# A gated linear attention block on one core: VectorE's order of weighing and gating keys, the bank of the turned decay rows, and ScalarE's place for the decay

## The chip, the cores and the metric

One core of one Trainium2 chip runs the whole program in one launch. The metric is device time in microseconds (us), the median of several executions. TensorE is called PE in the profile, with its weight loads as PEld; VectorE is DVE, ScalarE is ACT, GpSimd is POOL and SyncE, which issues most transfers, is SP.

## The reference

The block takes x of 8192 tokens by 512. The first half is normalised, modulated and sent through gated linear attention with 16 heads of 64; the second half is a gated feed-forward layer that mixes each token with the one before it. Only the first half is touched by the change.

```python
h = layernorm(x) * (1 + ca) + sa
q, k, v = h @ Wq.T, h @ Wk.T, h @ Wv.T
log_decay = -softplus(h @ Wd.T + bd)              # one number per token and head
k = k * sigmoid(h @ Wg.T)
s_t = exp(g_t) * s_{t-1} + k_t^T v_t ; o_t = q_t s_t   # per head, a 64 x 64 state
out = rmsnorm(o) * norm_w * sigmoid(h @ Wog.T) @ Wo.T
x = x + ga * out ; then x = x + gb * ffn(layernorm(x) * (1 + cb) + sb)
```

## The kernel before

The program has three parts that follow each other: `prepare` turns and splits the weights, `attention_pass` does everything up to `o`, and `output_pass` does the rest. Products of the projections are made in three passes, since each factor is split into a high and a low part (lines 55, 56 and 57 of the profile).

`attention_pass` works in 32 tiles of 256 tokens (two chunks of 128). Its turn i does two things side by side: the projections of tile i (`proj`), and the recurrence of tile j = i - 1 (`gla`). A turn has eight steps p = 0 to 7, one per pair of heads. Turn 0 has no recurrence (it also makes four modulation vectors), turns 1, 30 and 31 are written out, turns 2 to 29 are one hardware loop, and turn 32 has only the recurrence. So 31 turns have both.

In step p (1 to 7) PE turns the gated keys `kg` of pair p into `psX` (line 606), projects the gate `g` of pair p - 1 of the next tile, and ahead of the last quarter of that projection it waits in `ready()` for what the small products of the recurrence need, `kw` of pair p among it (`kv_ready`). Then come the small 64 x 64 products `weigh_v`, the state's increments, the scores and `add_held` (lines 570, 639, 648, 581), and then the projections of `q` and `k` of pair p - 1. The projections use the two banks `psJ` in turn, so each waits until the one two before it was read: `q` waits for DVE's reading of the `k` before it (`gate_k`, line 843), and `k` waits for ACT's reading of `g` (`copy_g`, line 720).

Each engine runs its own instructions in the order in which they are written; semaphores join them. DVE's step is `dve_tile`: `kw` (line 914, the turned keys weighed by a decay), `grow_q` (line 852), three `mid` and one `state` (line 929), `prob` (line 934), `sum_o` (line 889), and at the end `gate_k` of pair p - 1. ACT's step is `act_tile`: four exponentials (line 764), a copy of the state (`keep_state`, line 746), `copy_g`, `copy_o`, `copy_q`.

The decay of the next tile is made late in the turn. In step 6 PE sums the log decays into `psC` (lines 612 and 614), ACT makes `w_new` of it in `turn_decay` (lines 738 and 739), and PE turns two parts of `w_new` into rows, `psN`, inside the projection of `k` (line 538). DVE copies these rows out (line 954), SP stores them, and in step 7 reads them back, spread over the partitions, for the next turn (`spread_rows`, `grow_rows`). `psN` lies in `psP`, the banks from which DVE also reads `psO`; hence this wait of PE ahead of the projection of `k` in step 6:

```python
if p == 6:
    pe.wait_ge(s["w_new"], i + 1)
    if gla:
        hold(pe, s["o"], n)
project(i, "k", p - 1, pe, p == 6)
```

Of the kernel before, what the change touches and what calls it, by code (L numbers as in the profile page):

```python
# [26 lines left out]
H = 16  # L27
DH = HID // H
TOK = 8192
CH = 128  # L30
NC = 2
# [3 lines left out]
NP = HID // P  # L35
# [310 lines left out]
def attention_pass(nc, t, W, norm, h_parts, next_jobs, stage, h_next, h_loaded, wmod_v, x_v, o_v, h_v, cum_v, cum_b):  # L346
    with ExitStack() as ctx:  # L347
# [11 lines left out]
        o = sb("o", [P, 2, NC, CH])  # L359
# [28 lines left out]
        psP = ps("psP", [P, 2, 4, CH])  # L388
        psO, psN = psP[:, :, 0, :], psP[0:2 * NC * H, 0, 1, :]
        psJ = [ps(f"psJ{n}", [P, 512]) for n in range(2)]  # L390
        psT = ps("psT", [P, KD, T])
        psH = psP[:, :, 3, :]
        psC = psT[:, 1, NC * H:5 * NC * H]
        psM = psP[:, 1, 2, 0:KD]
# [45 lines left out]
        def grow_rows(sp, i, p):  # L440

            hold(sp, s["qg"], NP * i + p - 1)
            sp.dma_start(grown[:, p % 2, :],
                         cum_b[i, 1, 2 * p:2 * p + 2, :].unsqueeze(1).to_broadcast([2, DH, T])
                         ).then_inc(grow[p % 2], 16)
# [12 lines left out]
        def sp_tile(sp, i, gla, proj, prep, opens=False):  # L458
            j = i - 1
            for p in range(NP):  # L460
# [12 lines left out]
                if p == 7 and proj:  # L473
                    sp.wait_ge(s["n_rows"], 32 * (i + 1))
                    for pair in range(4):
                        spread_rows(sp, i, pair)
                    for pair in range(2):
                        grow_rows(sp, i, pair)
                if gla and (p > 0 or not opens):
                    store_o(sp, j if p else j - 1, (p - 1) % NP)  # L480
# [61 lines left out]
        def turn_x(pe, n):  # L542
            pe.wait_ge(s["xn"], NC * (n + 1))
            hold(pe, s["hT"], KD * n)
            hold(pe, s["w_new"], n - 1)
            for k in range(KD):
                for c in range(NC):
                    last = nc.tensor.transpose(psT[:, k, c * CH:(c + 1) * CH], x[:, c, k * P:(k + 1) * P],
                                               t["ident"][:, :])
                last.then_inc(s["xT"], 1)  # L550
# [43 lines left out]
        def pe_tile(pe, i, gla, proj, prep, opens=False):  # L594
            j = i - 1
            for p in range(NP):
# [22 lines left out]
                def ready():  # L619
                    if follows:  # L620
                        if p == 7 and proj:
                            pe.wait_ge(s["n_out"], i + 1)
                        o_ready(pe, n - 1)
                    kv_ready(pe, j, p)
# [34 lines left out]
                if p > 0 and proj:  # L659
                    project(i, "q", p - 1, pe)  # L660
                    if p == 6:
                        pe.wait_ge(s["w_new"], i + 1)
                        if gla:
                            hold(pe, s["o"], n)
                    project(i, "k", p - 1, pe, p == 6)
# [87 lines left out]
        def act_tile(act, i, gla, proj, prep, opens=False):  # L753
            j = i - 1
            for p in range(NP):
                n = NP * j + p
                if gla:
                    act.wait_ge(s["mask"], n + 1)
# [8 lines left out]
                    keep_state(act, j, p)  # L767
                    if p == 6 and proj:
                        turn_decay(act, i)
                    if p == 1:  # L770
# [122 lines left out]
        def dve_tile(dve, i, gla, proj, prep, opens=False):  # L893
            j = i - 1
            for p in range(NP):
# [13 lines left out]
                if gla:  # L909
                    if p == 0:  # L910
# [6 lines left out]
                        w_cur[:, 2, :, 2 * p:2 * p + 2].unsqueeze(3).to_broadcast([P, NC, 2, DH]),  # L917
                        ALU.mult).then_inc(s["kw"], 1)
                    grow_q(dve, j, p)
                    if not proj and p >= 3:  # L920
# [39 lines left out]
                if p == 5 and prep > 1:  # L960
                    norm_x(dve, i + 2)
                if p > 0 and proj:
                    gate_k(dve, i, p - 1)
            if proj:
                dve.wait_ge(s["w_new"], i + 1)
                hold(dve, s["state"], NP * i)
# [520 lines left out]
```

## Time and profile before

| what | value |
|---|---|
| time, median of 3 runs | 3450.75 us (3449.19 to 3459.34) |
| profiled execution, its own time | 3447.54 us |
| span of its trace | 3445.8 us |
| granted TensorE clock, mean over the span | 0.987 of full speed |
| busy: PE, DVE, ACT, POOL | 3288.3, 1888.0, 1308.6, 463.8 us |

The span is the time from the first to the last record of the trace, and 1.7 us of the profiled execution's own time lie outside it. Times in the rows below are counted from the start of the span. The attention part runs from about 46 us to about 2138 us; its turns 2 to 29 are about 64 us long each. Turn 4, from which most rows are taken, begins at 287.4 us and ends at 351.6 us.

### The profile page before, as it was taken

To read this page: it belongs to the slowest core of one execution; us is meant where nothing else is said; L and a number is where in the kernel's file an instruction comes from. 1 tells how busy PE (TensorE), PEld (TensorE's weight loads), DVE (VectorE), ACT (ScalarE), POOL (GpSimd) and SP (SyncE) were. 2 spreads that over 40 slices of the span, in tenths; PEclk is the share of its full clock that TensorE was granted. 3 is DMA by queue.
4 is the path that set the end of the run, shared out by engine and by line. 5 is a ranking of instruction groups with operands and counts; after the bars stand their busy time and mean duration, and the time that the engine had idled before them with its cause. 6 is when DMAs were issued, how large, how long until landed. Compare 5 with 4: busy or idle time off the path is not lost. (4 is left out here: it accounts for less than half of the span.)

```text
span 3445.8 us, 99642 instructions
## 1 busy us (share of the span) xinstructions
PE 3288.3 (95%) x37253; PEld 3015.9 (88%) x37253; DVE 1888.0 (55%) x4825; ACT 1308.6 (38%) x3584; POOL 463.8 (13%) x723
## 2 busy tenths in 40 slices
PE   7999999999999999999999997999999999999998
PEld 6888888898898888888888896888999988999887
DVE  6444444444444444444444445577676677676676
ACT  4344344344344344344344344323333323333322
POOL 0111101101111111101101111211121111121110
PEclk9999999999999999999999998999999999999999
DMA  5221221221221221221221224332222332222330
GB/s 202 80 83 64 84 80 62 76 89 63 84 81 63 81 83 64 84 80 62 77 88 62 83 70 144 98 85 73 73 77 81 87 84 73 73 78 80 87 83 25
DMA packets 273382, 279.77 MB, mean 81 GB/s; under 512 B 24720, under 2 KB 221344, under 8 KB 273072
## 3 DMA queue, kind: packets, MB, share of 16 engines
q1 hardware_dynamic: 270960, 270.67, 26.0%
q8 instruction: 290, 4.75, 0.6%
q10 hardware_dynamic: 2112, 4.19, 0.4%
q14 instruction: 20, 0.16, 0.0%
HBM read 189.84 MB, written 84.93 MB: 80 GB/s over the span
## 5 line engine op out<-in xcount | busy, mean ns | idle before, releaser
L55 PE MATMUL psJ<-h_hi,w_g_hi 128*128 128x256 f32 x1024 | 320.9, 313 | 36.5 <-DVE qg L852 30.5
L55 PE MATMUL psJ<-h_hi,w_q_hi 128*128 128x256 f32 x1024 | 309.1, 302 | 0.0
L55 PE MATMUL psJ<-h_hi,w_k_hi 128*128 128x256 f32 x1024 | 292.0, 285 | 12.4 <-DVE o L889 10.9
L929 DVE SCALAR_TENSOR_TENSOR mid<-state,w_all,psB 128x64 f32<-128x64 f32 x256 | 71.8, 280 | 414.5 <-PE psB L648 414.4
L55 PE MATMUL psG<-h_hi,w_og_hi 128*128 128x256 f32 x1024 | 287.6, 281 | 8.2 <-PEq L347 4.7
L57 PE MATMUL psJ<-h_hi,w_k_lo 128*128 128x256 f32 x1024 | 286.7, 280 | 0.0
L56 PE MATMUL psJ<-h_lo,w_g_hi 128*128 128x256 f32 x1024 | 286.7, 280 | 0.0
L56 PE MATMUL psJ<-h_lo,w_q_hi 128*128 128x256 f32 x1024 | 286.6, 280 | 0.0
L57 PE MATMUL psJ<-h_hi,w_q_lo 128*128 128x256 f32 x1024 | 286.4, 280 | 0.0
L56 PE MATMUL psJ<-h_lo,w_k_hi 128*128 128x256 f32 x1024 | 286.1, 279 | 0.0
L57 PE MATMUL psJ<-h_hi,w_g_lo 128*128 128x256 f32 x1024 | 285.8, 279 | 0.0
L56 PE MATMUL psG<-h_lo,w_og_hi 128*128 128x256 f32 x1024 | 284.6, 278 | 0.0
L57 PE MATMUL psG<-h_hi,w_og_lo 128*128 128x256 f32 x1024 | 284.5, 278 | 0.0
L764 ACT ACTIVATE prob<-cum_rows,w_cur 128x64 f32<-128x64 f32 x1024 | 273.6, 344 | 8.7 <-issue 4.9
L843 DVE SCALAR_TENSOR_TENSOR kg<-gate,psJ 128x256 f32<-128x256 f32 x256 | 107.8, 421 | 292.2 <-PE psJ L57 260.6
L55 PE MATMUL psJ<-w_v_hi,h_hi 128*128 128x264 f32 (+1 forms) x768 | 257.2, 335 | 0.4 <-DVE kg L843 0.4
L55 PEld LDWEIGHTS psJ<-h_hi,w_g_hi 128*128 128x128 f32 x1024 | 193.2, 189 | 72.8 <-issue 56.6
L57 PE MATMUL psJ<-w_v_hi,h_lo 128*128 128x264 f32 (+1 forms) x768 | 250.9, 327 | 0.0
L56 PE MATMUL psJ<-w_v_lo,h_hi 128*128 128x264 f32 (+1 forms) x768 | 250.0, 326 | 0.0
L720 ACT ACTIVATE gate<-psJ 128x256 f32<-128x256 f32 x256 | 98.5, 385 | 359.3 <-PE psJ L57 357.9
L751 ACT COPY o<-psP 128x256 f32<-128x256 f32 x256 | 95.1, 372 | 337.1 <-PE psP L581 333.8
L1223 ACT ACTIVATE og<-psG 128x512 f32<-128x512 f32 x128 | 76.7, 600 | 355.4 <-PE psG L57 355.3
(238 smaller groups left out, 9626.7 us busy)
## 6 DMA issues: line engine op xcount, KB each, us to landing
cum_rows<-cum_dram SPq DMA_DIRECT2D x512, 64.0 KB, 2.8
grown<-cum_dram SPq DMA_DIRECT2D x256, 128.0 KB
o_dram<-o SPq DMA_DIRECT2D x256, 128.0 KB, 1.9
o_cols<-o_dram SPq DMA_DIRECT2D x128, 256.0 KB, 5.0
an_norm_x<-in_L_attn_x_dram SPq DMA_DIRECT2D x32, 512.0 KB, 6.4
h_dram<-h_hi SPq DMA_DIRECT2D x32, 512.0 KB, 2.8
h_dram<-h_lo SPq DMA_DIRECT2D x32, 512.0 KB, 4.1
h_hi<-h_dram SPq DMA_DIRECT2D x32, 512.0 KB, 3.9
```

The costliest lines, as they stand in the source:

```text
L55: nc.tensor.matmul(out, w_hi, x_hi, start=first, stop=False)
L56: nc.tensor.matmul(out, w_hi, x_lo, start=False, stop=False)
L57: return nc.tensor.matmul(out, w_lo, x_hi, start=False, stop=last)
L720: nc.scalar.activation(gate[:, b % 2, :], psJ[USES.index(("g", b)) % 2][:, 0:T], ACT.Tanh, scale=0.5).then_inc(s["by_act"], 1)
L751: nc.scalar.copy(o[:, p % 2, :, :], psH).then_inc(s["o_part"], 1)
L764: last = nc.scalar.activation(prob[:, p % 2, 2 * h + c, :], rows_of(p)[:, h, c * DH:(c + 1) * DH], ACT.Exp, bias=w_cur[:, 0, c, 2 * p + h: ...
L843: nc.vector.scalar_tensor_tensor(out=kg[:, b, :], in0=gate[:, b % 2, :], scalar=1.0, in1=psJ[USES.index(("k", b)) % 2][:, 0:T], op0=ALU.ad ...
L929: nc.vector.scalar_tensor_tensor(out=into, in0=mid[:, p % 2, m - 1, :] if m else state[:, p, :], scalar=w_all[:, c, b, p:p + 1], in1=psK[: ...
L1223: nc.scalar.activation(og[:, n % 2, :, :], psG[n % 2][:, :].rearrange("p (b t) -> p b t", b=2), ACT.Sigmoid).then_inc(s["sg"], 1)
```

## The change

Four things change. DVE makes `kw` of pair p first and then gates the keys that PE projected in the step before, in steps 2, 3, 4, 6 and 7; the gating of pair 3 stays at the end of step 4, and those of pairs 6 and 7 at the end of the turn. `psN` moves from `psP` into `psT`, the banks in which x is turned; with it PE's wait for `o` in step 6 and its wait for `n_out` in step 7 go, and `turn_x` gets a wait for `n_out` of the turn before. ACT makes `w_new` ahead of step 6's exponentials in place of behind them and the state's copy. SP issues the reads of `grown` for pairs 0 and 1 between those of `cum_rows`.

```diff
@@ -386,10 +386,11 @@
         psS, psX = psB[:, :, 0, :], psB[:, 0, 2:4, :]
         psK = psB[:, :, 1, :].rearrange("p b (c d) -> p b c d", c=NC)
         psP = ps("psP", [P, 2, 4, CH])
-        psO, psN = psP[:, :, 0, :], psP[0:2 * NC * H, 0, 1, :]
+        psO = psP[:, :, 0, :]
         psJ = [ps(f"psJ{n}", [P, 512]) for n in range(2)]
         psT = ps("psT", [P, KD, T])
         psH = psP[:, :, 3, :]
+        psN = psT[0:2 * NC * H, 2, 0:CH]
         psC = psT[:, 1, NC * H:5 * NC * H]
         psM = psP[:, 1, 2, 0:KD]
 
@@ -472,10 +473,11 @@
                     sp.wait_ge(s["m_sum"], KD * len(MODS))
                 if p == 7 and proj:
                     sp.wait_ge(s["n_rows"], 32 * (i + 1))
-                    for pair in range(4):
+                    for pair in range(2):
                         spread_rows(sp, i, pair)
-                    for pair in range(2):
                         grow_rows(sp, i, pair)
+                    for pair in range(2, 4):
+                        spread_rows(sp, i, pair)
                 if gla and (p > 0 or not opens):
                     store_o(sp, j if p else j - 1, (p - 1) % NP)
                 if not proj and p == 0:
@@ -543,6 +545,7 @@
             pe.wait_ge(s["xn"], NC * (n + 1))
             hold(pe, s["hT"], KD * n)
             hold(pe, s["w_new"], n - 1)
+            hold(pe, s["n_out"], n - 1)
             for k in range(KD):
                 for c in range(NC):
                     last = nc.tensor.transpose(psT[:, k, c * CH:(c + 1) * CH], x[:, c, k * P:(k + 1) * P],
@@ -618,8 +621,6 @@
 
                 def ready():
                     if follows:
-                        if p == 7 and proj:
-                            pe.wait_ge(s["n_out"], i + 1)
                         o_ready(pe, n - 1)
                     kv_ready(pe, j, p)
 
@@ -660,8 +661,6 @@
                     project(i, "q", p - 1, pe)
                     if p == 6:
                         pe.wait_ge(s["w_new"], i + 1)
-                        if gla:
-                            hold(pe, s["o"], n)
                     project(i, "k", p - 1, pe, p == 6)
                 if p == 4 and proj:
                     for b in range(4):
@@ -754,6 +753,8 @@
             j = i - 1
             for p in range(NP):
                 n = NP * j + p
+                if p == 6 and proj and gla:
+                    turn_decay(act, i)
                 if gla:
                     act.wait_ge(s["mask"], n + 1)
                     hold(act, s["gla"], n - 1)
@@ -765,8 +766,6 @@
                                                         bias=w_cur[:, 0, c, 2 * p + h:2 * p + h + 1], scale=-1.0)
                     last.then_inc(s["e"], 1)
                     keep_state(act, j, p)
-                    if p == 6 and proj:
-                        turn_decay(act, i)
                     if p == 1:
                         copy_v(act, j, 5)
                 if p > 0 and proj:
@@ -916,6 +915,9 @@
                         psX.rearrange("p c (h d) -> p c h d", h=2),
                         w_cur[:, 2, :, 2 * p:2 * p + 2].unsqueeze(3).to_broadcast([P, NC, 2, DH]),
                         ALU.mult).then_inc(s["kw"], 1)
+                if proj and p > 1 and p != 5:
+                    gate_k(dve, i, p - 2)
+                if gla:
                     grow_q(dve, j, p)
                     if not proj and p >= 3:
                         rest_w(dve, p - 3)
@@ -959,9 +961,10 @@
                     norm_stats(dve, i + 2)
                 if p == 5 and prep > 1:
                     norm_x(dve, i + 2)
-                if p > 0 and proj:
+                if p == 4 and proj:
                     gate_k(dve, i, p - 1)
             if proj:
+                gate_k(dve, i, NP - 2)
                 dve.wait_ge(s["w_new"], i + 1)
                 hold(dve, s["state"], NP * i)
                 for h in range(2):
```

On DVE, in step 2 of a turn of the loop, these rows stand before: first the `kg` of the next tile's pair 0 and then the `kw` of pair 2, and `qg`.

```order
L840 ISA
L841 ISA [waits a_by_act]
L843 SCALAR_TENSOR_TENSOR kg<-gate,psJ 128x256 [waits a_score,a_proj]
L912 REGISTER_ALU
L914 TENSOR_TENSOR kw<-psB,w_cur 128x256 [waits a_inc,a_kT]
L849 REGISTER_ALU
L850 ISA [waits a_by_act]
L852 TENSOR_TENSOR qg<-q,grown 128x256 [waits a_gla,a_grow0]
```

After the change the same place reads:

```order
L911 REGISTER_ALU
L913 TENSOR_TENSOR kw<-psB,w_cur 128x256 [waits a_inc,a_kT]
L839 ISA
L840 ISA [waits a_by_act]
L842 SCALAR_TENSOR_TENSOR kg<-gate,psJ 128x256 [waits a_score,a_proj]
L848 REGISTER_ALU
L849 ISA [waits a_by_act]
L851 TENSOR_TENSOR qg<-q,grown 128x256 [waits a_gla,a_grow0]
```

The row of `kw` has moved ahead of that of `kg`; `qg` stays the third.

On ACT, in step 6 of a turn of the loop, these rows stand before. `prob` are the exponentials, `held` is the state's copy, `w_new` the decay, `gate` is what `copy_g` writes.

```order
L733 COPY q<-psJ 128x256 [waits a_qg,a_score,a_proj]
L758 REGISTER_ALU
L764 ACT_TABLE_LOAD [waits a_gla]
L764 ACTIVATE prob<-cum_rows,w_cur 128x64 [waits a_mask]
L764 ACTIVATE prob<-cum_rows,w_cur 128x64 x3
L746 COPY held<-state 128x64 [waits a_gla,a_state]
L738 ACTIVATE w_new<-psT 128x32 [waits a_cur,a_cum]
L739 ACTIVATE w_new<-psT 128x128
L718 REGISTER_ALU
L45 REGISTER_ALU [waits a_proj]
L720 ACTIVATE gate<-psJ 128x256 [waits a_k]
```

After the change, from the same place:

```order
L732 COPY q<-psJ 128x256 [waits a_qg,a_score,a_proj]
L737 ACTIVATE w_new<-psT 128x32 [waits a_cur,a_cum]
L738 ACT_TABLE_LOAD
L738 ACTIVATE w_new<-psT 128x128
L759 REGISTER_ALU
L765 ACTIVATE prob<-cum_rows,w_cur 128x64 [waits a_gla,a_mask]
L765 ACTIVATE prob<-cum_rows,w_cur 128x64 x3
L745 COPY held<-state 128x64 [waits a_gla,a_state]
L717 REGISTER_ALU
L45 REGISTER_ALU [waits a_proj]
L719 ACTIVATE gate<-psJ 128x256 [waits a_k]
```

The two rows of `w_new`, with the wait for PE's sums (`a_cum`), have moved from behind `held` to ahead of the exponentials, and the load of the activation table has moved with them: it stands between the two.

In turn 0, which makes the modulation vectors, DVE's rows of steps 1 and 2 stand like this before. `m_sums` is a sum over weight rows of 128 x 512, and `kg` here is pair 0.

```order
L865 SCALAR_TENSOR_TENSOR m_sums<-m_rows,c_silu_c,m_sums 128x512 [waits a_m_sum] x3
L843 SCALAR_TENSOR_TENSOR kg<-gate,psJ 128x256 [waits a_proj,a_by_act]
L871 COPY c_mod<-psP 128x4 [waits a_m_read]
L876 TENSOR_SCALAR sign<-c_mod 128x4 [waits a_m_out]
L877 SCALAR_TENSOR_TENSOR sign<-c_mod 128x4
L880 TENSOR_SCALAR sign<-sign 128x4 [waits a_gate]
L881 TENSOR_SCALAR sign<-sign 128x4
L883 TENSOR_TENSOR c_ga<-sign 128x4 [waits a_gate]
L862 TENSOR_SCALAR m_sums<-cum_rows,c_silu_c 128x512 [waits a_m_read,m_loaded1,a_gate]
L865 SCALAR_TENSOR_TENSOR m_sums<-cum_rows,c_silu_c,m_sums 128x512 [waits a_m_sum] x3
L843 SCALAR_TENSOR_TENSOR kg<-gate,psJ 128x256 [waits a_proj,a_by_act]
```

After the change:

```order
L864 SCALAR_TENSOR_TENSOR m_sums<-m_rows,c_silu_c,m_sums 128x512 [waits a_m_sum] x3
L870 COPY c_mod<-psP 128x4 [waits a_m_read]
L875 TENSOR_SCALAR sign<-c_mod 128x4 [waits a_m_out]
L876 SCALAR_TENSOR_TENSOR sign<-c_mod 128x4
L879 TENSOR_SCALAR sign<-sign 128x4 [waits a_gate]
L880 TENSOR_SCALAR sign<-sign 128x4
L882 TENSOR_TENSOR c_ga<-sign 128x4 [waits a_gate]
L861 TENSOR_SCALAR m_sums<-cum_rows,c_silu_c 128x512 [waits a_m_read,m_loaded1,a_gate]
L864 SCALAR_TENSOR_TENSOR m_sums<-cum_rows,c_silu_c,m_sums 128x512 [waits a_m_sum] x3
L842 SCALAR_TENSOR_TENSOR kg<-gate,psJ 128x256 [waits a_proj,a_by_act]
```

The `kg` of pair 0 has moved from ahead of the second sum `m_sums` to behind it. The same happens in steps 5 and 6 with the `kg` of pair 4.

## Rows read from the trace of the kernel before

**Rows 1.** The page, its first part: busy time, share of the span, instructions.
```profile
PE 3288.3 (95%) x37253; PEld 3015.9 (88%) x37253; DVE 1888.0 (55%) x4825; ACT 1308.6 (38%) x3584; POOL 463.8 (13%) x723
```

**Rows 2.** PE's waits, 290 to 2055 us: total us, times, longest.
```profile
PE psB L606 <- issue: 52.2, 25, 2.6
PE psJ L55 <- DVE qg L852: 26.8, 55, 0.5
PE psJ L55 <- DVE o L889: 10.1, 26, 0.4
```

**Rows 3.** Timeline, PE's weight loads, step 2: start, us, engine, line, what.
```profile
303.04 0.19 PEld L56 LDWEIGHTS psJ<-h_lo,w_g_hi 128*128 128x128 f32 x1
303.16 0.19 PEld L57 LDWEIGHTS psJ<-h_hi,w_g_lo 128*128 128x128 f32 x1
303.49 0.19 PEld L55 LDWEIGHTS psJ<-h_hi,w_g_hi 128*128 128x128 f32 x1
```

**Rows 4.** Timeline, PE and DVE, step 2 of the same turn.
```profile
302.12 0.38 PE L606 MATMUL psB<-c_ident,kg 128*128 128x128 f32 x2
...
302.31 0.42 DVE L843 SCALAR_TENSOR_TENSOR kg<-gate,psJ 128x256 f32<-128x256 f32 x1 [1.34 <-PE psJ L57]
302.65 0.42 DVE L914 TENSOR_TENSOR kw<-psB,w_cur 128x256 f32<-128x256 f32 x1
```

**Rows 5.** Timeline, PE and DVE, turn 32, where no keys are gated.
```profile
2099.93 0.38 PE L606 MATMUL psB<-c_ident,kg 128*128 128x128 f32 x2
...
2100.35 0.42 DVE L914 TENSOR_TENSOR kw<-psB,w_cur 128x256 f32<-128x256 f32 x1 [0.72 <-PE psB L606]
```

**Rows 6.** Timeline, DVE and PE's weight loads, step 6.
```profile
337.08 0.41 DVE L889 TENSOR_TENSOR o<-o,psP 128x256 f32<-128x256 f32 x1
...
336.96 0.19 PEld L57 LDWEIGHTS psJ<-h_hi,w_q_lo 128*128 128x128 f32 x1
337.73 0.19 PEld L55 LDWEIGHTS psJ<-h_hi,w_k_hi 128*128 128x128 f32 x1 [0.59 <-issue]
```

**Rows 7.** Groups, 290 to 2055 us: busy, mean ns, idle before, releaser.
```profile
L55 PEld LDWEIGHTS psJ<-h_hi,w_k_hi 128*128 128x128 f32 x872 | 165.3, 190 | 15.5 <-issue 15.5
```

**Rows 8.** Timeline, PE and ACT, step 6.
```profile
332.84 0.41 PE L614 MATMUL psT<-g_half,c_ones 128*128 128x64 f32 x2
...
331.04 0.37 ACT L733 COPY q<-psJ 128x256 f32<-128x256 f32 x1 [0.32 <-PE psJ L57]
331.43 1.28 ACT L764 ACT_TABLE_LOAD   x1
332.72 1.07 ACT L764 ACTIVATE prob<-cum_rows,w_cur 128x64 f32<-128x64 f32 x4
333.70 0.23 ACT L746 COPY held<-state 128x64 f32<-128x64 f32 x1
...
333.92 0.26 ACT L739 ACTIVATE w_new<-psT 128x128 f32<-128x128 f32 x1
334.79 0.39 ACT L720 ACTIVATE gate<-psJ 128x256 f32<-128x256 f32 x1 [0.61 <-PE psJ L57]
```

**Rows 9.** Timeline, DVE and PE's weight loads, turn 0.
```profile
56.30 2.33 DVE L865 SCALAR_TENSOR_TENSOR m_sums<-cum_rows,c_silu_c,m_sums 128x512 f32<-128x512 f32 x3
...
56.04 0.19 PEld L55 LDWEIGHTS psJ<-h_hi,w_q_hi 128*128 128x128 f32 x1
...
81.79 0.42 DVE L843 SCALAR_TENSOR_TENSOR kg<-gate,psJ 128x256 f32<-128x256 f32 x1
...
82.64 2.33 DVE L865 SCALAR_TENSOR_TENSOR m_sums<-cum_rows,c_silu_c,m_sums 128x512 f32<-128x512 f32 x3
...
84.43 0.19 PEld L55 LDWEIGHTS psJ<-h_hi,w_q_hi 128*128 128x128 f32 x1
```

**Rows 10.** Windows: stretch, us, busy of five engines, granted clock, DMA share, GB/s.
```profile
416.90:420.30 3.40, 3.40 (x10) 2.55 (x8) 0.43 (x1) 0.00 (x0) 0.00 (x0) 0.52 0.24 74
1840.30:1843.70 3.40, 3.40 (x10) 2.62 (x9) 0.82 (x2) 0.00 (x0) 0.00 (x0) 0.51 0.29 79
```

## The prediction

> **What bounds the kernel now.** I read the page first: PE is busy for 95% of the span and every other engine for 55% or less [rows 1]. So the time is PE's work plus what PE waits for, and a change that leaves its products alone can only win back waits. The view of PE's waits says which they are in the hardware loop [rows 2]: a stop at the loop's restart that nothing in the profile ends (52.2 us), 55 waits named after `qg` (two a turn, in steps 1 and 5, where DVE does other work ahead of `kw`), and 26 of 0.4 us named after DVE's `sum_o`, one a turn. The change touches the last kind. It does not touch the restart, nor steps 1 and 5, whose order on DVE stays.
>
> That view misses short stops, because it takes each product as busy for 0.28 us although the next starts after 0.12. The timeline of the weight loads shows them: they come 0.12 us apart, and in step 2 one comes at 303.49 where 303.28 was due [rows 3], a stop of 0.21 us ahead of the last quarter of the projection of `g`, where PE waits for `kw`. Steps 3, 4 and 7 have the same. In step 6 the first load of the projection of `k` comes at 337.73 where 337.08 was due, 0.65 us late [rows 6].
>
> **The change part by part. PE's wait for `o` in step 6** goes. `sum_o` ends at 337.49 and the load follows at 337.73, so 0.24 us is what a hand-over from DVE to this load takes [rows 6]. With `psN` in another bank, only the decay and ACT's reading of `g` are left to wait for. The decay was ready at 334.18 [rows 8], the rest is below. If neither is late, the whole 0.65 us is won. It is no feature of one turn: the weight loads of `k` stand idle for 15.5 us ahead of their start between 290 and 2055 us, 0.57 us in each of 27 turns [rows 7], and a load's own 0.19 less the spacing of 0.12 makes it 0.64. For 31 turns: 31 x 0.65 = 20.2 us.
>
> **`kw` ahead of `kg` in steps 2, 3, 4 and 7.** In step 2 the two turning products start at 302.12, `kg` occupies DVE from 302.31, and `kw` starts at 302.65, 0.53 us behind the products [rows 4]. Where no keys are gated, `kw` starts 0.42 us behind them [rows 5]. So `kw` is held up for 0.11 us by `kg`, not for its whole 0.42, because the turning itself lasts nearly as long. The stop of 0.21 us shrinks by that and does not vanish; unrounded the two rows differ by slightly more, and I take 0.12. 31 x 4 x 0.12 = 14.9 us. The bounds are 0 (the wait is ended by something other than `kw`, so 0 us) and 0.21 (it ends the stop, 26 us); the hand-over is the nearer evidence. In step 6 the small sums of the decay come between the turning and the projection and cover `kw`, so nothing is won there. `kg` itself comes 0.34 us later and `qg` 0.2 us; `kg` is needed by the projection of `q`, which comes behind the rest of `g`'s and all the small products, and `qg` in the next step, so both cost nothing.
>
> **ACT makes the decay ahead of the exponentials.** This is where something can be lost, since ACT now waits for PE's sums. Before, it loaded the table at 331.43, right behind the copy of `q`, while it had nothing else to do, and the exponentials, the state's copy, the decay and `gate` followed [rows 8]. After, the load stands behind an instruction that waits for the sums. The last of the two L614 products starts about 0.14 us behind the row's 332.84, and with 0.3 us from a product's start to the reader's (as from the second turning product, 0.11 behind 2099.93, to `kw` at 2100.35 [rows 5]) that instruction starts at 333.3. It takes 0.19 us, the load 1.28, so the second starts near 334.8, the exponentials near 334.95, the state's copy near 335.93 and `gate` near 336.06, ending at 336.45, in place of 335.18. PE wants it for the bank of the projection of `k`, due at 337.08; less the hand-over of 0.24 there are 0.39 us to spare. DVE waits for the state's copy ahead of `mid`: it ends at 336.16, which makes `prob` of step 6 about 0.6 us late, near 337.8, and PE asks for it only behind the projection of `k`, after 338.5. So I cost this edit at nothing, and the cover is 0.39 us thin.
>
> The Trainium skill, on its page "ScalarE: Activation LUTs", section "What ACT_TABLE_LOAD costs", puts a switch of tables at 1283 ns plus a drain of about 1380 ns. The load in the trace takes 1.28 us, which agrees, but the exponentials start 0.01 us behind it and it starts 0.02 us behind the copy of `q`, so no drain of that size stands beside it here [rows 8].
>
> **Turn 0 loses.** There DVE gates pair 0 behind a sum over weight rows. That sum ends at 58.63, `kg` would end 0.33 later at 58.96, and with 0.24 for the hand-over PE can load `q` at 59.20; it did at 56.04 [rows 9]. 3.2 us. Pair 4: the sums start at 81.79 in place of `kg`'s, end 0.33 earlier than before at 84.64, `kg` ends at 84.97, PE loads at 85.21 in place of 84.43: 0.8 us. Between them DVE's row of pair 1 may cost some 0.2. Together 4.2 us, once.
>
> **`grown` ahead of `cum_rows` on SP.** Two issues move ahead by some transfers, so `qg` of step 0 is earlier. PE's waits name no such transfer in any turn [rows 2], since step 1 waits for the low part of h, which follows the last projection of `v`. Pair 1's rows are read one issue later and have a step to spare. Nothing. The waits for `n_out`, moved by a turn, were long over: nothing. The transfers that DVE's copy of the decay rows releases start 0.65 us earlier within the turn, ahead of a whole turn's use.
>
> **Sum.** 20.2 + 14.9 - 4.2 = 30.9 us. From the profiled execution's 3447.5 this gives 3416.6. That execution lay 3.2 us under the median, so from the median it is 3419.9. I say 3418, between the two.
>
> **The rivals.** First, **`kw` was not what the short stop waited for**: then it stays, the gain is 20.2 - 4.2 = 16.0, the time 3434. For it: the profile names `qg` in steps 1 and 5, not `kw`. Against: `qg` of that step isn't needed until the next one, and the distances fit `kw`.
>
> Second, the mirror of it: **the stop goes altogether**, 26 in place of 14.9, time 3407. For it: `kw` ends 0.11 us earlier and the restart after a stop may be cheaper. Against: 0.1 us is left by the rows.
>
> Third, **ACT is late in step 6 after all**. Each tenth beyond the 0.39 us costs 3.1 us. If as much as one more load's time, 1.28 us, stood in the chain, PE would stop for 0.89 us: 27.6 us, and the time would be 3446, no change. By the skill's 1.38 us of drain it would be 31 x 0.99 = 30.7, about 3449.
>
> Fourth, **slower**: the same mechanism with the table loaded twice round the moved instructions, 2.56 us more. Then PE stops for 2.17 us a turn, 67 us, and the time is 3485. It decides from a lateness of 0.39 + 1.34 = 1.7 us on. Against it: the built order shows one load a turn in step 6, as before.
>
> Fifth, **the clock**. After some restarts of the loop the granted clock falls to 1.2 GHz, as at 416.9 and 1840.3, the first and last of 8 among 27 [rows 10]. A stretch of 3.4 us at half of 2.4 GHz gives back at most 1.7 us. The stop ahead of it isn't changed, so I expect as many; three more or fewer are 5 us either way, which is in the range. If all 27 restarts fell so, 32 us would be lost and the gain with it.
>
> **How the numbers follow.** The forecast has 0.60. No gain from `kw` 0.12, the whole stop 0.09, ACT late by about a load 0.08, ACT late by more 0.03, the clock 0.03, something else, mostly near no change, 0.05. The range goes from the whole stop (3407, less some noise) to no gain from `kw` with a few us of the clock: 3405 to 3438. A measurement of this kernel tells 0.3%, 10.4 us, from no change, so faster means under 3440. Faster: 0.60 + 0.12 + 0.09 and, of ACT late by a load, the clock and the rest (0.16 together), the 0.07 in which only part of the gain is lost, 0.88; same: the other 0.09; slower: 0.03.
>
> **What would show it.** In the profile after: no wait of PE on `sum_o` ahead of `k`; the weight load of `k` in step 6 0.12 us behind the one before; `kw` 0.42 us behind the first turning product and ahead of `kg`; the short stop in step 2 about 0.1 us; ACT's table load behind the sums and `gate` ending some 0.6 us ahead of that load; `grown` no longer waited for as long by DVE; a stop of about 3 us in turn 0 ahead of `q`. Wrong would be a wait of PE for `gate` in step 6, or a gap in step 2 as long as before.

## The result and the profile after

The changed kernel takes 3459.1 us (median of 20 runs, 3452.9 to 3464.4), the kernel before beside it 3452.9 us (20 runs). The ratio is 1.0018, with a 95% interval of 1.0011 to 1.0025: a loss of 6 us, small but clear of the noise, where a gain of 31 us was forecast.

The page's row of busy times after the change (engine, busy us, share of the span, instructions), to be held against [rows 1]:

```profile
PE 3291.0 (95%) x37253; PEld 3028.0 (88%) x37253; DVE 1873.0 (54%) x4825; ACT 1301.1 (38%) x3584; POOL 464.1 (13%) x723
```

PE's waits of the changed kernel, 290 to 2055 us (total us, times, longest):

```profile
PE psB L609 <- issue: 70.0, 26, 3.2
PE psJ L55 <- DVE qg L851: 25.8, 55, 0.5
```

The wait for `o` is gone, as forecast, and `qg` stands where it stood. The stop at the loop's restart, which the forecast left alone, has grown from 52.2 to 70.0 us [rows 2].

The steps that were priced did happen. Timeline of the changed kernel, step 6 of turn 4, ACT, DVE and PE's weight loads, to be read beside [rows 6, 8]:

```profile
339.44 0.20 ACT L737 ACTIVATE w_new<-psT 128x32 f32<-128x32 f32 x1 [1.83 <-PE psT L617]
339.65 1.28 ACT L738 ACT_TABLE_LOAD   x1
340.94 0.28 ACT L738 ACTIVATE w_new<-psT 128x128 f32<-128x128 f32 x1
341.11 1.05 ACT L765 ACTIVATE prob<-cum_rows,w_cur 128x64 f32<-128x64 f32 x4
342.07 0.23 ACT L745 COPY held<-state 128x64 f32<-128x64 f32 x1
342.20 0.38 ACT L719 ACTIVATE gate<-psJ 128x256 f32<-128x256 f32 x1
...
343.11 0.19 PEld L57 LDWEIGHTS psJ<-h_hi,w_q_lo 128*128 128x128 f32 x1
343.23 0.19 PEld L55 LDWEIGHTS psJ<-h_hi,w_k_hi 128*128 128x128 f32 x1
```

The weight load of `k` follows 0.12 us behind the last of `q`; it was 0.77. ACT's `gate` ends at 342.58, 0.65 us ahead of that load: the chain that the forecast drew for ACT (0.63 expected) holds.

In step 2 (timeline, PE's weight loads and DVE, beside [rows 3, 4]):

```profile
308.68 0.38 PE L609 MATMUL psB<-c_ident,kg 128*128 128x128 f32 x2
...
309.10 0.42 DVE L913 TENSOR_TENSOR kw<-psB,w_cur 128x256 f32<-128x256 f32 x1 [1.56 <-PE psB L609]
...
309.73 0.19 PEld L57 LDWEIGHTS psJ<-h_hi,w_g_lo 128*128 128x128 f32 x1
309.95 0.19 PEld L55 LDWEIGHTS psJ<-h_hi,w_g_hi 128*128 128x128 f32 x1
```

`kw` starts 0.42 us behind the turning products, where it took 0.53, and the last quarter's first load is 0.10 us late in place of 0.21.

**Where the time went.** I split each turn of the hardware loop, in the trace, into the stop at the restart (from the start of the last product of a turn to that of the first of the next), the head (from there to `turn_x`, about 7 us) and the rest, and took means over the 27 restarts (26 turns for the rest):

| us | stop | head | rest | turn | falls of the clock |
|---|---|---|---|---|---|
| before | 2.34 | 7.59 | 54.76 | 64.67 | 8 |
| after | 2.96 | 8.58 | 53.48 | 65.02 | 26 |

A fall is a restart with a stretch at the lower granted clock (1.2 GHz) that begins between 1.2 us ahead of the stop's end and 3 us behind it. The rest is 1.28 us shorter (forecast: 0.65 + 4 x 0.12 = 1.13). The stop gives back 0.62, and the head 0.99: before, a head without a fall takes 7.2 us on average (7.0 to 7.7), and one with a fall takes 8.6 in both kernels. All these figures, here and below, come from one profiled execution of each kernel; that of the kernel before was 5.4 us shorter than the median of its 20 runs. Between the two profiled executions: 28 x 1.28 = 35.8 us won in the loop and 4.8 in turns 1, 30 and 31; lost are 27 x 0.62 = 16.7 at the stops, 27 x 0.99 = 26.7 in the heads, and 7.1 in turn 0. That sums to 9.9 us slower; the spans differ by 9.7.

### The profile page after: what moved, and what is told of

It reads as the page before. It is cut to its first block and busy times, and to the rows that moved or that the text cites. A ratio compares the mean times of both kernels' runs of the same rounds, so it can differ in the third digit from the quotient of the medians.

```text
span 3455.5 us, 99585 instructions
## 1 busy us (share of the span) xinstructions
PE 3291.0 (95%) x37253; PEld 3028.0 (88%) x37253; DVE 1873.0 (54%) x4825; ACT 1301.1 (38%) x3584; POOL 464.1 (13%) x723
## 5 line engine op out<-in xcount | busy, mean ns | idle before, releaser
L55 PE MATMUL psJ<-w_v_hi,h_hi 128*128 128x264 f32 (+1 forms) x768 | 268.9, 350 | 0.4 <-DVE kg L842 0.4
L57 PE MATMUL psJ<-w_v_hi,h_lo 128*128 128x264 f32 (+1 forms) x768 | 260.8, 340 | 0.0
L56 PE MATMUL psJ<-w_v_lo,h_hi 128*128 128x264 f32 (+1 forms) x768 | 260.6, 339 | 0.0
L913 DVE TENSOR_TENSOR kw<-psB,w_cur 128x256 f32<-128x256 f32 x256 | 108.2, 423 | 247.0 <-PE psB L609 247.0
```

Of the source, the lines that this page charges most:

```text
L55: nc.tensor.matmul(out, w_hi, x_hi, start=first, stop=False)
L56: nc.tensor.matmul(out, w_hi, x_lo, start=False, stop=False)
L57: return nc.tensor.matmul(out, w_lo, x_hi, start=False, stop=last)
L913: nc.vector.tensor_tensor(kw[:, :, :].rearrange("p c (h d) -> p c h d", h=2), psX.rearrange("p c (h d) -> p c h d", h=2), w_cur[:, 2, :, 2 ...
```

## The restart of the loop

Timeline of the kernel before at the restart behind turn 4, SP's issues and PE's products:

```profile
341.87 6.25 SPq L436 DMA_DIRECT2D cum_rows<-cum_dram  x8
348.31 1.29 SPq L443 DMA_DIRECT2D grown<-cum_dram  x2
...
349.45 0.28 PE L57 MATMUL psJ<-h_hi,w_k_lo 128*128 128x256 f32 x1
351.56 0.41 PE L606 MATMUL psB<-c_ident,kg 128*128 128x128 f32 x2 [1.83 <-issue]
```

The changed kernel, the restart behind turn 5:

```profile
412.73 1.42 SPq L437 DMA_DIRECT2D cum_rows<-cum_dram  x2
414.40 0.57 SPq L444 DMA_DIRECT2D grown<-cum_dram  x1
415.21 1.43 SPq L437 DMA_DIRECT2D cum_rows<-cum_dram  x2
416.84 0.55 SPq L444 DMA_DIRECT2D grown<-cum_dram  x1
417.57 4.74 SPq L437 DMA_DIRECT2D cum_rows<-cum_dram  x4
...
419.48 0.28 PE L57 MATMUL psJ<-h_hi,w_k_lo 128*128 128x256 f32 x1
422.81 0.41 PE L609 MATMUL psB<-c_ident,kg 128*128 128x128 f32 x2 [3.05 <-issue]
```

"issue" means that no semaphore held PE. What PE waits for shows in the DMA view, as a queue of its own kind. Queues of the kernel before, 348.5 to 351.6 us (packets, MB, share of 16 engines' time):

```profile
q1 hardware_dynamic: 417, 0.29, 30.1%
q8 instruction: 1, 0.02, 2.1%
```

The changed kernel, 418.5 to 421.5 us:

```profile
q1 hardware_dynamic: 401, 0.25, 26.6%
q8 instruction: 1, 0.02, 5.0%
```

At a restart one packet of 16 KB with instructions is fetched. Before it takes 0.021 x 3.1 x 16 = 1.0 us, after 0.050 x 3.0 x 16 = 2.4 us, with no more data moved beside it. Over 27 restarts the first fetch at each takes 0.98 us on average before and 1.58 after, 0.60 more, and the stop is 0.62 longer.

That the stop is this fetch can be read restart by restart. In all 27 restarts of each of the two kernels PE's first product starts 1.63 to 1.80 us behind the end of the fetch (mean 1.70 before, 1.71 after). The fetch begins on average 0.35 us ahead of the turn's last product before and 0.32 after. So only its length differs: 0.88 to 1.30 us before; after the change 2.1 to 2.5 us at 11 restarts, where the stop is 3.1 to 3.5, and 0.9 to 1.6 at the other 16.

What differs is what is in flight: the last read of `grown` is issued 0.4 us ahead of the turn's last product before and 2.6 us ahead of it after (medians of 27). In the 1.5 us ahead of the fetch no packet of 1 KB, the size of `grown`'s, starts at any restart before, and 49 to 72 start at each after. Such a read moves slowly; in the kernel before, 350.0 to 350.9 us, hardly anything else runs (the view's line of the total, then the queue's):

```profile
DMA packets 48, 0.05 MB, mean 50 GB/s; under 512 B 1, under 2 KB 48, under 8 KB 48
...
q1 hardware_dynamic: 48, 0.05, 16.1%
```

48 packets of 1 KB in 0.9 us keep 16.1% of 16 engines, 2.6 of them, busy. `grown` is read with an access pattern whose outermost step counts 2 (two heads, each spread over 64 partitions). The Trainium skill says on its page "DMA: Bandwidth & Descriptors", section "Rules for kernel authors", that the slowest dimension larger than 1 sets how many engines a transfer uses, so that an outermost count of c under 16 keeps it on at most c. The trace agrees in so far as 2.6 of 16 engines are busy with it. That the fetch queues behind such a row of packets on one of these engines is my reading: the trace doesn't name the engine of a packet. The Trainium skill's page "Runtime: NRT & Kernel Launch", section "Instruction fetch mechanics", says that a taken branch to a page that isn't held forces a fetch before execution goes on. The trace agrees: 16 KB are fetched at each restart, and PE stops for 2.34 us on average even in the kernel before.

## The experiments

The expectations name theories by letters: A, that SP's reads start too late and run into the restart; B, that the clock falls by where the restarts lie in time; C, that the order of SP's reads does the harm. Experiments named after_ start from the changed kernel, before_ from the kernel before. The ratio is to the kernel before on the same chip.

**after_sp**: SP's reads in their old order.

```diff
-                    for pair in range(2):
+                    for pair in range(4):
                         spread_rows(sp, i, pair)
+                    for pair in range(2):
                         grow_rows(sp, i, pair)
-                    for pair in range(2, 4):
-                        spread_rows(sp, i, pair)
```

> The changed kernel with SP's order of reads as before (eight of cum_rows, then the two of grown). Theory A (late store): the first read still starts late, so the restart is disturbed as much: 3455 to 3462. Theory C (the order itself: cum_rows as the last reads hurts the instruction fetch, grown does not): the fetch takes 0.9 us again at all restarts and the time falls to about 3430.

Measured 3424.8 us, ratio 0.9912 (0.9892 to 0.9932), 34 us under the changed kernel. PE's waits in it, 290 to 2055 us:

```profile
PE psB L608 <- issue: 53.0, 25, 2.6
```

The stop is 2.38 us, falls 13, the rest 53.55. So the new order on SP, priced at "Nothing", cost all of the expected gain. The expectation had the reason the wrong way round: it blamed the reads of `cum_rows`, and after_split below points at `grown`.

**after_cum**: the store of the decay rows ahead of that of `o`.

```diff
+                if p == 6 and proj:
+                    sp.wait_ge(s["n_out"], i + 1)
+                    for b in range(2):
+                        sp.dma_start(cum_v[i, :, b, :, :], cum_out[:, b * DH:(b + 1) * DH]).then_inc(s["n_rows"], 16)
                 if gla and (p > 0 or not opens):
                     store_o(sp, j if p else j - 1, (p - 1) % NP)
-                if p == 6 and proj:
-                    ...
```

> The changed kernel, but in step 6 SP stores the decay rows ahead of o of the step before, not behind it. Theory A (contention): the stop at the loop's restart grew because SP's reads of cum_rows now run into it; they start late because the store of the decay rows stands directly behind the 128 KB store of o (reads follow 3.4 us behind the store's issue, before 1.4 us). Then the reads start 1 to 2 us earlier, end ahead of the restart as before, the stop falls from 3.0 to 2.3 us a turn and the granted clock falls after fewer restarts: 3459 less 27 x 0.65 = 17 and less up to 1.4 for each fall that stays away: 3415 to 3442. Theory B (phase alone): the clock falls because of where the restarts lie in time, not because of the stop's length: the time stays within 5 us of 3459 unless the turn's length changes.

Measured 3466.4 us, ratio 1.003 (1.0018 to 1.0042); stop 3.12, falls 25. The first read starts 7.4 us ahead of the turn's last product in place of 6.8 (medians of 27), and nothing is won. That is 0.6 us of the 1 to 2 that were expected, so the run speaks against a late store as the cause, but weakly; after_sp and after_split decide.

**after_turn0**: turn 0 gates its keys where it did before.

```diff
-                if proj and p > 1 and p != 5:
+                if proj and gla and p > 1 and p != 5:
                     gate_k(dve, i, p - 2)
 ...
-                if p == 4 and proj:
+                if proj and (p == 4 if gla else p > 0):
                     gate_k(dve, i, p - 1)
             if proj:
-                gate_k(dve, i, NP - 2)
+                if gla:
+                    gate_k(dve, i, NP - 2)
```

> The changed kernel with the gating of keys in turn 0 where it was before. Both theories: turn 0 lasted 66.4 us in place of 59.3; it gets back 7 us, so 3452. Under theory B the later turns may lie otherwise against the clock; a difference beyond 7 us either way speaks for it.

Measured 3452.0 us, ratio 0.999 (0.998 to 1.000): turn 0 is 5.1 us shorter than in the changed kernel (61.3 for 66.4), and a fall follows each of the 27 restarts. Its profiled execution was the slowest of the 12, at 3459.3 us.

**before_psn**: the kernel before with `psN` in `psT` and the waits changed with it, as in the diff of the change; DVE's, ACT's and SP's orders as before.

> The kernel before with only the decay rows moved to the other bank and the waits of PE that go with it. The step 6 stop of 0.65 us a turn goes (20 us), nothing in turn 0, nothing on ACT. If a stop taken from PE is simply won: 3433. Theory A: here sum_o is not late and its store keeps its distance only partly, since the decay rows come 0.6 us earlier and their store moves up to the store of o; so part is lost at the restart: 3430 to 3450. Theory B: depends on the turn's length of about 64.0 less 0.65 us without falls; falls after many restarts and 3440 to 3455.

Measured 3442.4 us, ratio 0.996 (0.9947 to 0.9973). The rest is 53.97, 0.79 us less than before (0.65 forecast); the stop 2.42, falls 17.

**before_sp**: the kernel before with SP's new order alone (the first diff of this section turned round).

> The kernel before with SP's new order of reads alone (grown of pairs 0 and 1 between the reads of cum_rows). Theory C (the order: the second read of grown is now in flight while PE fetches instructions at the loop's restart, a fetch takes 2.2 us in place of 0.9, and the longer stop brings the clock down after nearly every restart): as between after and after_sp, 34 us slower than the kernel before: 3475 to 3495. Rival (the order hurts only together with the decay rows' store, which the bank's move puts right behind the store of o): in the kernel before the reads start 2 us earlier, the reads are over at the restart, and the time stays at 3450 to 3458.

Measured 3456.9 us, ratio 1.001 (1.000 to 1.0019). PE's waits in it, 290 to 2055 us:

```profile
PE psB L607 <- issue: 71.1, 26, 3.2
```

The stop is 3.00 us as in the changed kernel, so the order makes the stop by itself. But only 12 restarts have a fall, and the time rises by 3 us where 27 x 0.66 = 18 would be due and 3475 to 3495 us were expected. Its profiled execution, from which the stops and falls are read, was the slowest of its 12 at 3468.6 us, 21 us over that of the kernel before; over the 12 the mean granted clock is 0.9882 against 0.9870 beside it. That makes up some 4 us (0.0012 of 3457) of the missing 15, and the rest I can't account for. So the order alone brings the longer stop, and what it costs in time depends on the rest of the change.

**after_split**: each read of `grown` issued as two, one for each head, spread over 64 partitions.

```diff
-            sp.dma_start(grown[:, p % 2, :],
-                         cum_b[i, 1, 2 * p:2 * p + 2, :].unsqueeze(1).to_broadcast([2, DH, T])
-                         ).then_inc(grow[p % 2], 16)
+            for h in range(2):
+                sp.dma_start(grown[h * DH:(h + 1) * DH, p % 2, :],
+                             cum_b[i, 1, 2 * p + h, :].unsqueeze(0).to_broadcast([DH, T])
+                             ).then_inc(grow[p % 2], 16)
```

> The changed kernel, SP's order as changed, but each read of grown is made in two halves of 64 partitions, whose outermost step is 64 and not 2. In the trace the packets of grown leave 24 in half a microsecond at 46 ns each, as if two of the 16 DMA engines took them all in turn; split, all 16 should share them. Theory C in this form (a fetch that shares one of two long queues waits): fetches take 0.9 to 1.2 us, the stop falls to 2.3 to 2.6 us, fewer falls of the clock, 3420 to 3440. Rival (any reading by SP during the restart lengthens it, and there are four more issues a turn): 3455 to 3475.

Measured 3426.4 us, ratio 0.992 (0.9906 to 0.9934). With SP's new order kept, the stop is 2.40 us and the fetch 0.99 us on average, 1.34 at most, although packets of 1 KB still start around each of the 27 fetches. The same bytes do not lengthen the stop once each read is made as two, of 64 partitions each. (The last of them is issued 1.1 us ahead of the turn's last product, not 2.6, since SP has more to issue.) Falls are 20 of 27 here.

Not all of the 33 us are won at the restarts. Turn 32, which has only the recurrence, lasts 40.1 us in place of 45.9. In the changed kernel DVE's `qg` waits 6.0 us there for reads of `grown`:

```profile
DVE qg L851 <- DMA grown<-cum_dram: 6.0, 2, 5.6
```

In after_split the view of the same turn has no such row. Behind the attention both kernels take as long (1306.9 and 1306.8 us).

**after_pad12, after_pad4, after_pad24**: the changed kernel with m = 12, 4, 24 repeated turning products ahead of those of `turn_x`.

```diff
             hold(pe, s["n_out"], n - 1)
+            for _ in range(m):
+                nc.tensor.transpose(psT[:, 0, 0:CH], x[:, 0, 0:P], t["ident"][:, :])
             for k in range(KD):
```

> The changed kernel with twelve more turning products of x on PE in every turn ahead of its turning of x (they write what is written again), 12 x 0.11 = 1.3 us a turn, 41 us over all turns. Theory A/C (the length of the stop decides whether the clock falls): the falls stay after nearly every restart, 3495 to 3502. Theory B (the turn's length of 65 us puts every restart in the same place against the clock's steps): another length scatters them, about half of the falls go, 27 x 0.5 x 1.4 = 19 us are won back: 3475 to 3485.

> The changed kernel with 4 turning products of x repeated in each turn. Twelve of them made the turn's part behind the restart 0.66 us longer, so four are priced at 0.2 us, 31 times 7 us. If the nearly unbroken row of falls of the clock (26 of 27 restarts) belongs to one length of the turn, this one, 65.2 us, has them still or begins to lose them; time 3459 to 3470. If they come from the length of the stop alone, there are 26 again, 3466.

> The same with 24 repeated products: 24 in place of 12 add about 0.12 us each where nothing covers them, 1.4 us to the 0.66, so 2.1 us a turn and 64 us in all, 3523, if the clock falls as often as in the changed kernel. If falls belong to a length of the turn, there are under 15 of 27 here as with 12 (16), and the time is some 15 us less, 3508. The stop at the restart should stay at 3.0 us.

Measured 3474.6, 3461.9 and 3509.9 us, ratios 1.0057 (1.004 to 1.0073), 1.0024 (1.0014 to 1.0034) and 1.0159 (1.0142 to 1.0176). The twelve products are not 1.3 us of the turn, as I had taken, but 0.66 (rest 54.14); a part of them lies in time in which PE waited anyway (its waits named after `qg` come to 14.0 us in place of 25.8). Falls are 27 with 4, 15 with 12 and 18 with 24, of 27 each, at stops of 3.12, 3.14 and 3.11 us; fewer than 15 had been expected with 24.

**best**: the changed kernel with SP's old order and turn 0's old gating. From it: **best_kg**, DVE gating ahead of weighing again; **best_act**, ACT's decay behind the exponentials again; **best_pad12**, twelve products more.

> The changed kernel with SP's reads in the order of before and turn 0's gating as before: what is left are the parts that the forecast priced (31 x 0.65 us and 31 x 4 x 0.12 us). The forecast's own terms without turn 0 give 35 us under before, ratio 0.990. My theory (the reads of grown in flight at the restart, and the clock) says the kernel with SP's old order was 30 us under before and turn 0 gives 5 more: 35 us, ratio 0.990, with 12 to 17 falls of the clock in 27 restarts and a stop of 2.3 to 2.5 us. The rival, that the change's own edits on DVE or ACT bring the falls by another way, gives the same time with over 20 falls only if the steps gained more than priced.

> The kernel best with DVE gating the keys ahead of weighing them, as before; ACT's decay stays ahead of the exponentials. The forecast's term for the order of kw says 31 x 4 x 0.12 = 14.9 us more than best. If that term is right the part of a turn behind the projections' start grows by 0.48 us; if kw is not what the short stop waits for, by 0. The clock can move the total by some 5 us either way (about 1.5 us for each restart more or fewer with a fall).

> The kernel best with ACT's decay behind step 6's exponentials and the state's copy, as before. The forecast's term for ACT is nothing, so the same time as best within 0.15%. The rival is that the early decay makes step 6 late (prob and mid wait for it): then this is up to 10 us faster than best. The other rival is that it is of use, because SP's store and reads of the decay come 0.65 us earlier and are clear of the restart: then the stop at the restart is longer here, 2.4 to 3.0 us, and the time up to 15 us more than best.

> The kernel best with 12 turning products of x repeated in each turn, 1.3 us of PE's time, as in the changed kernel with the same 12 (there 31 x 1.3 = 41 us of work cost 15 us). If a turn's work and the falls of the clock are independent, it costs 41 us over best: ratio to before 1.002. If whether the clock falls at a restart hangs on how long a turn is, a longer turn than the changed kernel's 65.0 us has fewer falls: then 66 us turns here have fewer than best's and the padding costs 20 to 35 us, with under 12 falls of 27.

| kernel | us | ratio | stop | rest | falls |
|---|---|---|---|---|---|
| best | 3424.8 | 0.9917 (0.9898 to 0.9935) | 2.39 | 53.59 | 16 |
| best_kg | 3431.3 | 0.9931 (0.9919 to 0.9944) | 2.27 | 53.95 | 11 |
| best_act | 3432.7 | 0.9935 (0.9922 to 0.9948) | 2.47 | 53.59 | 19 |
| best_pad12 | 3445.5 | 0.9977 (0.9969 to 0.9986) | 2.15 | 54.21 | 8 |

`best` was expected 35 us under the kernel before and is 29. It is no faster than after_sp (ratio 0.9912), from which it differs by turn 0's gating alone, though that was worth 7 us in after_turn0; no run explains this. The order of `kw` is worth 0.36 us a turn (0.48 forecast), ACT's order 0.00 in the rest of the turn, as forecast. The 8 us of best_act (5 at most were expected) lie in stops and falls, and its interval overlaps that of best. Twelve products cost 21 us here and 15 in the changed kernel, where their 0.62 and 0.66 us a turn come to 19 and 20. So the 41 us that I had put on them were too many, and I drop the reading that the falls swallowed most of that.

**before_two, after_two, best_two**: two turns in each pass of the hardware loop, on every engine, so 12 restarts between passes in place of 27.

```diff
-            with pe.Fori(2, NT - 2) as i:
+            with pe.Fori(2, NT - 4, 2) as i:
                 pe_tile(pe, i, True, True, 2)
+                pe_tile(pe, i + 1, True, True, 2)
+            pe_tile(pe, NT - 4, True, True, 2)
+            pe_tile(pe, NT - 3, True, True, 2)
```

> The kernel before with two turns in each pass of the hardware loop (its turns 2 to 27 in 13 passes, 28 and 29 written out), so 12 restarts lie between passes in place of 27. Where a pass runs on from one turn to the next, the stop of about 2.3 us should be absent. 15 stops fewer at 2.3 us are 35 us; with the falls of the clock that follow a restart, 35 to 45 us: 3410 to 3420.

> The changed kernel with two turns in each pass. If the loss of the changed kernel is at the restarts (a stop of 3.0 us and a fall of the clock after nearly each), it loses 15 of them at 3.0 and 1.6 us: about 70 us, 3390. Then the change beats the kernel before where both have two turns a pass, by some 15 to 30 us, though it is 4 to 6 us slower with one. If the loss were spread over the turn, both would gain alike and the changed kernel would stay the slower.

> The changed kernel with SP's order and turn 0's gating as before, and with two turns in each pass of the hardware loop (26 turns in 13 passes, turns 28 and 29 written out), so 12 restarts in place of 27. If each restart costs its 2.3 us of stop and about half of them a fall of the clock of 1.4 us: 15 x (2.2 + 0.7) = 43 us below 3421: 3375 to 3390. If the fetching of instructions is as slow without a jump (the stop is the fetch itself, not the jump), little is won: 3410 to 3425.

PE's waits, 290 to 2055 us, in before_two:

```profile
PE psB L609 <- issue: 21.8, 11, 2.6
```

and in after_two:

```profile
PE psB L612 <- issue: 34.6, 12, 3.1
```

before_two takes 3414.5 us (ratio 0.9886, 0.987 to 0.9903), after_two 3384.5 (0.9799, 0.9783 to 0.9816), best_two 3388.8 (0.981, 0.9791 to 0.9829). In the middle of a pass no stop of over 0.6 us shows at a turn's start in any of the three. With two turns a pass the same change that lost 6 us wins 30. The restarts, not the turns, ate the gain. best_two should beat after_two, by its shorter stops and turn 0, and doesn't: their intervals overlap, and I can't say which is faster.

## Why the prediction was wrong

- **PE's wait for `o` in step 6, 31 x 0.65 = 20.2 us**: right. before_psn shows 0.79 us a turn, and the load follows 0.12 us behind the one before.
- **`kw` ahead of `kg`, 31 x 4 x 0.12 = 14.9 us**: right in mechanism, some high in size. The stop shrank and did not vanish: between best_kg and best the late loads of the four steps together go from 0.94 to 0.47 us a turn, where 0.48 less had been forecast. Of that, the rest of the turn gives back 0.36 us, 11 us in all.
- **ACT at nothing**: right. `gate` is 0.65 us ahead of the load, and best_act has the same rest as best. No drain shows beside the table load here either: `w_new` starts 0.01 us behind it.
- **Turn 0, 4.2 us**: the stop was right and the total too small, 7.1 us. PE loads `q` at 59.04 (59.20 forecast):

```profile
56.33 2.33 DVE L864 SCALAR_TENSOR_TENSOR m_sums<-cum_rows,c_silu_c,m_sums 128x512 f32<-128x512 f32 x3
58.57 0.41 DVE L842 SCALAR_TENSOR_TENSOR kg<-gate,psJ 128x256 f32<-128x256 f32 x1
59.04 0.29 PEld L55 LDWEIGHTS psJ<-h_hi,w_q_hi 128*128 128x128 f32 x1 [2.90 <-DVE kg L842]
```

  Behind it the granted clock is low, at 1.2 GHz: the loads that follow come 0.21 us apart, not 0.12. The windows of turn 0's first step (us, busy of PE, PEld, DVE, ACT, POOL, granted clock, DMA share, GB/s), after:

```profile
46.30:66.42 20.12, 16.73 (x95) 16.34 (x96) 10.84 (x31) 3.14 (x7) 0.69 (x1) 0.70 0.77 270
```

  and before:

```profile
46.30:59.32 13.02, 12.53 (x84) 12.33 (x85) 10.26 (x27) 3.17 (x7) 0.69 (x1) 0.79 0.94 331
```

- **"`grown` ahead of `cum_rows` on SP ... Nothing"**: this is the step that failed. I looked for a wait of PE that names such a transfer, found none, and priced the edit by that. The only wait that it reaches is the one put down to "issue", the restart, of which I had written that the change does not touch it. The fetch of instructions stands in the DMA view beside the data, and with the second read of `grown` issued 2.6 us ahead of the turn's last product, in place of 0.4, it takes 1.58 us in place of 0.98: 27 x 0.62 = 17 us of stop. after_sp and after_split take it back by two different edits.
- **The clock, "the stop ahead of it isn't changed, so I expect as many"**: wrong with the step above. The case that I gave 0.03 is what came about, 26 falls for 8. A fall makes a head 1.4 us longer by the means (8.6 and 7.2), near the bound of 1.7, and the heads cost 27 us in all.

**What stays open** is why the clock falls at nearly every restart, and with it the cause of the 27 us in the heads. The new order on SP has its part in it: falls go from 26 to 13 without it (after_sp). Within each kernel that has restarts of both kinds, the stops with a fall are the longer ones on average (before: 2.57 us with, 2.24 without). But the stop's length alone doesn't do it: before_sp has 12 falls at a mean of 3.00 us, after_pad12 15 at 3.14, and in the changed kernel 15 of the 16 restarts whose fetch was short had a fall as well. Nor does the turn's: best_pad12 has 8 at 64.4 us, of which a turn with a fall lasts 2.15 + 8.6 + 54.21 = 65.0. All four kernels with one turn a pass and 25 or more falls of 27 (after, after_turn0, after_cum, after_pad4) have both, a stop of 3.0 to 3.1 us and, reckoned in the same way, a turn of 65.0 to 65.2 us; with such a stop and turns of 65.9 to 67.1 (after_pad12, before_sp, after_pad24) it is 12 to 18. That is a pattern in seven kernels and not a cause shown.

## What to carry to other kernels

In this kernel a wait put down to "issue" at a loop's restart was a wait for a fetch of instructions, so an edit to the order of transfers around it had a price though no engine waited for those transfers. Look at the DMA view's instruction queue (share x window x 16 is the time of a fetch), keep transfers whose outermost count is small clear of the restart, or issue them so that this count is larger, as after_split did. Before polishing steps of 0.1 us in a loop's body, halve its restarts: here that was worth 37 us in the kernel before and some 75 in the changed one.

## What the runs showed of the hardware

- A restart of this loop stops PE until 1.6 to 1.8 us behind the end of a 16 KB fetch of instructions: for 1.7 to 2.8 us in the kernel before (fetches of 0.9 to 1.3 us), and for 3.1 to 3.5 where the fetch takes 2.1 to 2.5 us (11 restarts after the change).
- With two transfers to 64 partitions each the fetch took 0.99 us on average, with one whose outermost count is 2 it took 1.58 (after_split and after).
- The granted clock after a restart is 2.4 GHz or falls to 1.2 GHz for a stretch; the head then takes 8.6 us in place of 7.2. How often it does so varies from 8 to 27 of 27 restarts between the profiled executions, which can move the time by 27 us (19 x 1.4): a smaller gain that is spread over this loop can't be read from the total alone.
